# Attention kernel: differences by slot group, and sums of exponentials added up on VectorE before the denominators

## The chip, the cores and the metric

The kernel runs on one core of a Trainium2 chip. The metric is the device time of one execution in microseconds. The engines are named as in the profile: PE is the matrix engine (its weight loads are listed as PEld), DVE is VectorE, ACT is ScalarE, POOL is GpSimd and SP is the queue that issues most transfers.

## The reference

The whole program is a small audio layer. 128 batches of 64 features by 750 samples are pooled in windows of 8 to 94 tokens; then come a layer norm, an attention with 8 heads of width 8, and a feed-forward part with experts. The change lies in the attention alone. Cut to that:

```
qgr, _ = jnp.linalg.qr(q)
kgr, _ = jnp.linalg.qr(k)
attn_grass = jnp.einsum('bhnd,bhmd->bhnm', qgr, kgr) ** 2 * grassman_scale
dots = jnp.einsum('bhnd,bhmd->bhnm', q, k)
attn_eucl = dots * scale
attn_riem = dots ** 2 * riem_scale
a = jnp.concatenate([attn_eucl, attn_riem, attn_grass], axis=1)
...
a = jnp.einsum('oc,bcnm->bonm', conv_w, a) + conv_b[None, :, None, None]
a = jax.nn.softmax(a, axis=-1)
out = jnp.einsum('bhnm,bhmd->bhnd', a, v)
```

Three kinds of scores (24 channels) are mixed to 8, and a softmax over the keys follows. What matters here is the end of it: subtract a maximum, take exponentials, sum them over the keys (the denominators), multiply with v, and divide.

## The kernel before

The attention is the function `attend`. It works on pairs of batches, 64 pairs, one pair in a step. Each engine has its own program, written out by hand, and the five run beside each other; semaphores alone tie them. The order on each engine is that of its `step` function. PE's steps are all written out; the others have a loop of two steps a round.

The keys of a batch are laid out on 128 partitions (16 keys by 8 heads) in 6 slots, so the scores of a pair are `[128 partitions, 2 batches, 6 slots, 94 queries]`, all in f32. They lie in PSUM in `ps_a`, four banks: two for each batch, with slots 0 to 2 in one bank and 3 to 5 in the other. The parts of a step i are spread over three pairs:

- PE: `dots` of pair i in three groups (L1064), with `turn_keys` of pair i+2 (L1050) and `turn_max` of pair i-1 (L1071) behind the first group, `spread_max` of pair i-1 (L1077) behind the second, then `attended` (L1088) and `denominators` (L1095) of pair i-2, the third group, and `linear` (L1107) and `mixing` (L1115) of pair i, which fill `ps_a`.
- ACT: the squares of the dots (L1165), and between them the exponentials of pair i-1 (L1159 for slots 0 to 3, L1160 for slots 4 and 5, which has another bias), once for each batch.
- DVE: `maxima` of pair i-1 (`row_max`, L1188, once for each batch), `heads_max` (L1200, L1202), then the shift (L1206) and the two differences `prob` = `ps_a` - `shift` (L1211, one for each batch, 564 elements a partition), then `output` of pair i-2 (a reciprocal and a product, L1216 and L1218) and `key_blocks` of pair i+2 (L1195).
- POOL: `halves` (L1012) adds slots 0 to 2 to slots 3 to 5 of the exponentials of one pair, which leaves `half`, `[128, 2, 3, 94]`; then the key tiles (L1019, L1021), `m_blk` (L1005) and `v_blk` (L997).

The denominators are the sums over the partitions and over the three slots that are left. PE makes both in one: three matmuls a batch with `den_w`, which accumulate in PSUM. `linear` overwrites `ps_a`, so it waits for both differences of the pair before (`sub_done`).

Of the kernel before, what the change touches and what calls it, by code (L numbers as in the profile page):

```python
# [516 lines left out]
def later(c, behind):  # L517

    return not isinstance(c, int) or c >= behind
# [407 lines left out]
def attend(nc, q_cm, k_cm, m_t, o_cm, v_dram, k):  # L927
# [2 lines left out]
    SLOTS = 4  # L930
    with ExitStack() as ctx:
        names = ("m_ready keys_ready turned_ready mix_ready v_ready kt_done dots_done squared keyed mixed "
                 "max_done max_turned max_heads max_ready max_spread shift_done sub_done exp_done half_done av_done inv_done out_done")
        s = {n: ctx.enter_context(sem(n)) for n in names.split()}
        v_in = [ctx.enter_context(sem(f"v_in{a}")) for a in range(2)]
        q_in = [ctx.enter_context(sem(f"q_in{a}")) for a in range(2)]
# [14 lines left out]
        shift = sb("shift", [128, 2, N])  # L951
        prob = sb("prob", [128, 2, 2, NT, N])
        half = sb("half", [128, 2, 3, N])
        inv = sb("inv", [128, N])
        ps_dot = ctx.enter_context(nc.psum_tensor("ps_dot", [128, 3, 512], F32))
        ps_a = ctx.enter_context(nc.psum_tensor("ps_a", [128, 4, 512], F32))
        ps_m = ctx.enter_context(nc.psum_tensor("ps_m", [128, 512], F32))
        AV_AT, DEN_AT, KT_AT, REST = 0, N, 2 * N, 3 * N
        block = ctx.enter_context(nc.Block())

        def steps(eng, step):
# [28 lines left out]
        @block.gpsimd  # L990
        def _(pool):
            def values(j, a, n):
                pool.wait_ge(v_in[a], 32 * n)
                if later(j, 2):
                    pool.wait_ge(s["av_done"], j - 1)
                for b in range(2):
                    vb = pool.tensor_tensor(v_blk[:, a, b].rearrange("p t (o d) -> p (t o) d", o=H),  # L997
                                            v_rep[:, a, b].rearrange("p (t o d) -> p (t o) d", o=H, t=NT),
                                            k["vmask"][:].rearrange("p t o -> p (t o)").unsqueeze(2).broadcast_to([128, NT * H, D]), ALU.mult)
                vb.then_inc(s["v_ready"], 1)  # L1000

            def turning(i, a):
                if later(i, 2):
                    pool.wait_ge(s["kt_done"], i - 1)
                pool.tensor_tensor(m_blk[:, a], m_t[:, span(i, 1), :].broadcast_to([128, 16, D]),  # L1005
                                   k["mask16"][:].unsqueeze(2).broadcast_to([128, 16, D]), ALU.mult).then_inc(s["m_ready"], 1)

            def halves(j, a):
                pool.wait_ge(s["exp_done"], 2 * j + 2)
                if later(j, 1):  # L1010
                    pool.wait_ge(s["av_done"], j)
                pool.tensor_tensor(half[:], prob[:, a, :, 0:3, :], prob[:, a, :, 3:6, :], ALU.add).then_inc(s["half_done"], 1)  # L1012

            def build(i, a, n, has_next2):
                if later(i, 3):
                    halves(i - 3, 1 - a)
                if later(i, 2):
                    pool.wait_ge(s["keyed"], 2 * (i - 1))
                pool.tensor_tensor(k_blk[:, a, :, 0], k_cm[:, span(i, 1), :].rearrange("p i (u m) -> p (i u) m", m=4).unsqueeze(2).broadcast_to([128, NT * SLOTS, H, 4]),  # L1019
                                   k["hmask"][:].unsqueeze(1).unsqueeze(3).broadcast_to([128, NT * SLOTS, H, 4]), ALU.mult).then_inc(s["keys_ready"], 1)  # L1020
                pool.tensor_tensor(k_mix[:, a].rearrange("p t x o -> p (t x) o"), k_cm[:, span(i, 1), :].rearrange("p i m -> p (i m)").unsqueeze(2).broadcast_to([128, NP, H]),  # L1021
                                   k["conv1"].unsqueeze(1).broadcast_to([128, NP, H]), ALU.mult).then_inc(s["mix_ready"], 1)
                if has_next2:
                    turning(i + 2, a)
                if later(i, 1):
                    values(i - 1, 1 - a, n)

            turning(0, 0)
            turning(1, 1)
            for i in range(4):  # L1030
                build(i, i % 2, (i + 1) // 2, True)
            with pool.Fori(2, PAIRS // 2 - 1) as twice:
                build(2 * twice, 0, twice, True)
                build(2 * twice + 1, 1, twice + 1, True)
            build(PAIRS - 2, 0, PAIRS // 2 - 1, False)
            build(PAIRS - 1, 1, PAIRS // 2, False)
            halves(PAIRS - 3, 1)
            values(PAIRS - 1, 1, PAIRS // 2)
            halves(PAIRS - 2, 0)
            halves(PAIRS - 1, 1)  # L1040

        @block.tensor
        def _(pe):
# [45 lines left out]
                                  start=(t == 0), stop=(t == NT - 1), skip_group_check=True)  # L1089

            def denominators(j):
                pe.wait_ge(s["half_done"], j + 1)
                for t in range(3):
                    for b in range(2):
                        mm = pe.matmul(ps_m[64 * b:64 * b + 64, DEN_AT:DEN_AT + N], k["den_w"][:], half[:, b, t, :],  # L1095
                                       start=(t == 0), stop=(t == 2), skip_group_check=True)
                mm.then_inc(s["av_done"], 1)

            def linear(i, a):
                if later(i, 1):  # L1100
                    pe.wait_ge(s["sub_done"], 2 * i)
                pe.wait_ge(s["mix_ready"], i + 1)
                for t in range(NT):
                    for b in range(2):
                        for w in range(2):
                            half_of = slice(64 * w, 64 * w + 64)
                            mm = pe.matmul(ps_a[half_of, 2 * b + t // 3, N * (t % 3):N * (t % 3) + N],  # L1107
                                           k_mix[64 * b:64 * b + 64, a, t, 8 * w:8 * w + 8].rearrange("p x o -> p (x o)"), q_st[64 * b:64 * b + 64, a, :],
                                           start=(t % 3 == 0), stop=False, skip_group_check=True)
                        if t == NT - 1:  # L1110
                            mm.then_inc(s["keyed"], 1)

            def squares_mixed(i, b, v):
                for c in range(SLOTS):
                    mm = pe.matmul(ps_a[32 * c:32 * c + 32, 2 * b + v, 0:3 * N], k["mix_w"][64 * v:64 * v + 64, :],  # L1115
                                   sq[64 * v:64 * v + 64, b, c].rearrange("p t n -> p (t n)"), start=False, stop=True, skip_group_check=True)
                return mm

# [35 lines left out]

        @block.scalar
        def _(act):
            def exps(prev, a, b):
                act.wait_ge(s["sub_done"], 2 * prev + b + 1)
                act.activation(prob[:, a, b, 0:4], prob[:, a, b, 0:4], ACT.Exp, bias=k["head_const"][:])  # L1159
                act.activation(prob[:, a, b, 4:6], prob[:, a, b, 4:6], ACT.Exp, bias=k["pad_bias"][:]).then_inc(s["exp_done"], 1)  # L1160

            def squares(i, g):
                act.wait_ge(s["dots_done"], 3 * i + g + 1)
                for b in range(2):
                    act.activation(sq[:, b, :, g, :], ps_dot[:, (2 * g + b) % 3, 0:SLOTS * N].rearrange("p (c n) -> p c n", c=SLOTS),  # L1165
                                   ACT.Square).then_inc(s["squared"], 1)

            def step(i, a, has_prev, has_prev2, has_next2):
                if has_prev:
                    act.wait_ge(s["mixed"], 2 * i)  # L1170
                squares(i, 0)
                squares(i, 1)
                if has_prev:
                    exps(i - 1, 1 - a, 0)
                squares(i, 2)
                if has_prev:
                    exps(i - 1, 1 - a, 1)

            steps(act, step)
            for b in range(2):  # L1180
                exps(PAIRS - 1, 1, b)

        @block.vector
        def _(dve):
# [19 lines left out]
            def shifted(prev, a):  # L1204
# [2 lines left out]
                dve.wait_ge(s["shift_done"], prev + 1)  # L1207
                if later(prev, 2):
                    dve.wait_ge(s["av_done"], prev - 1)
                for b in range(2):  # L1210
                    dve.tensor_tensor(prob[:, a, b].rearrange("p (v t) n -> p v t n", v=2), bass.AP(ps_a[:].tensor, 1024 * b, [[4 * 512, 128], [512, 2], [N, 3], [1, N]]),  # L1211
                                      shift[:, b, :].unsqueeze(1).unsqueeze(1).broadcast_to([128, 2, 3, N]), ALU.subtract).then_inc(s["sub_done"], 1)

            def output(j):
                dve.wait_ge(s["av_done"], j + 1)
# [4 lines left out]
            def step(i, a, has_prev, has_prev2, has_next2):  # L1220
                if has_prev:
                    maxima(i - 1)
                if has_prev:
                    heads_max(i - 1)
                    shifted(i - 1, 1 - a)
                if has_prev2:
                    output(i - 2)
# [6 lines left out]
            maxima(PAIRS - 1)  # L1234
            heads_max(PAIRS - 1)
            shifted(PAIRS - 1, 1)
            output(PAIRS - 2)
            output(PAIRS - 1)


def finish(nc, h, o_cm, out, k):
# [288 lines left out]
```

## Time and profile before

| | us |
|---|---|
| median of 3 runs | 924.77 |
| lowest and highest | 920.41, 924.92 |
| the profiled execution, in all | 921.8 |
| its span in the trace | 920.1 |
| the attention, first to last `row_max` in the trace | 316.1 to 781.7 |

The profile is of one execution. It lists each engine's busy time, the groups of instructions by line with what ended the idle time before them, and a timeline. Durations are those of single instructions; consecutive instructions on an engine can overlap by some hundredths of a microsecond. A matmul of f32 is recorded as two passes, so 6 matmuls stand there as x12. "128x94 f32<-128x564 f32" reads output and input, partitions by elements.

### The profile page before, as it was taken

The page shows a single profiled execution, that of the slowest core. Times are in us where ns is not written, and L with a number is a line of the kernel's source. Part 1 is how long each engine was busy: PE and PEld are TensorE (multiplying, and loading weights), DVE is VectorE, ACT ScalarE, POOL GpSimd, SP SyncE. Part 2 cuts the span into 40 slices and gives each one's busy share as a digit, 9 for nine tenths or more (in the row PEclk, how much of TensorE's full clock was granted, in tenths as well). Part 3 has the DMA queues.
Part 4 walks back from the last instruction along what each step waited for, and adds up shares of the span by engine and source line. Part 5 has one row for each costly group of instructions (what it writes and reads, how often), then busy time and mean ns, then how long its engine had stood idle before and what let it go on. Part 6 is the DMA issues. An engine that isn't in the chain of part 4 may idle for free. (4 is left out here: it accounts for less than half of the span.)

```text
span 920.1 us, 40061 instructions
## 1 busy us (share of the span) xinstructions
PE 812.1 (88%) x16806; PEld 580.0 (63%) x16806; DVE 678.7 (74%) x1163; ACT 452.4 (49%) x966; POOL 506.6 (55%) x551
## 2 busy tenths in 40 slices
PE   3577768899895699999999999999999999699994
PEld 2233325455553577887888877777888877366663
DVE  4488894488799577777787877777787877377772
ACT  2233333211282265555565655555565655277773
POOL 3256570121000688888888888888888886222220
PEclk9678888799998699999999999999999999799998
DMA  8667200022410122222111222222221111001111
GB/s 291 264 219 250 69 1 0 12 60 50 113 48 0 60 62 63 65 71 66 61 61 62 61 62 63 67 68 66 61 62 61 61 62 42 1 18 28 29 28 33
DMA packets 64293, 64.92 MB, mean 71 GB/s; under 512 B 36825, under 2 KB 54812, under 8 KB 64156
## 3 DMA queue, kind: packets, MB, share of 16 engines
q1 hardware_dynamic: 63628, 61.24, 21.4%
q8 instruction: 124, 2.03, 0.9%
q10 hardware_dynamic: 528, 1.54, 0.5%
q14 instruction: 13, 0.11, 0.0%
HBM read 52.93 MB, written 6.75 MB: 65 GB/s over the span
## 5 line engine op out<-in xcount | busy, mean ns | idle before, releaser
L1165 ACT ACTIVATE sq<-ps_dot 128x376 f32<-128x376 f32 x384 | 165.2, 483 | 160.5 <-PE ps_dot L1064 160.5
L1064 PE MATMUL ps_dot<-q_st,k_blk 64*64 64x94 f32 x6144 | 170.5, 249 | 1.1 <-ACT sq L1165 0.8
L1064 PEld LDWEIGHTS ps_dot<-q_st,k_blk 64*64 64x64 f32 x6144 | 134.6, 134 | 53.0 <-issue 28.8
L997 POOL TENSOR_TENSOR v_blk<-v_rep,vmask 128x384 f32<-128x384 f32 x128 | 106.6, 854 | 27.4 <-PE ps_m L1095 27.4
L1012 POOL TENSOR_TENSOR half<-prob 128x564 f32<-128x564 f32 x64 | 75.6, 1181 | 61.0 <-ACT prob L1160 61.0
L1188 DVE TENSOR_REDUCE row_max<-ps_a 128x94 f32<-128x564 f32 x128 | 89.4, 740 | 24.0 <-PE ps_a L1115 24.0
L1159 ACT ACTIVATE prob<-prob,head_const 128x376 f32<-128x376 f32 x128 | 78.0, 609 | 57.0 <-DVE prob L1211 57.0
L1019 POOL TENSOR_TENSOR k_blk<-k_cm,hmask 128x768 f32<-128x768 f32 x64 | 96.8, 1513 | 1.0 <-PE ps_a L1107 1.0
L1021 POOL TENSOR_TENSOR k_mix<-k_cm,cols 128x768 f32<-128x768 f32 x64 | 96.8, 1513 | 0.0
L1211 DVE TENSOR_TENSOR prob<-ps_a,shift 128x564 f32<-128x564 f32 x128 | 89.4, 740 | 4.9
L367 PE MATMUL ps_spread<-parts,pair_sel 128*128 128x376 bf16 x256 | 58.1, 368 | 34.7 <-DVE prod L477 22.8
L1115 PE MATMUL ps_a<-sq,mix_w 64*32 64x282 f32 x2048 | 82.0, 404 | 0.1
L436 POOL TENSOR_TENSOR prod<-x_g,w_odd 128x752 f32<-128x752 f32 x32 | 56.9, 1778 | 39.1 <-ACT w_odd L419 39.1
L1088 PE MATMUL ps_m<-prob,v_blk 128*64 128x94 f32 x1536 | 76.6, 248 | 1.5 <-ACT prob L1160 1.5
L1107 PE MATMUL ps_a<-q_st,k_mix 64*64 64x94 f32 x3072 | 74.8, 241 | 1.2 <-DVE prob L1211 0.9
L1297 POOL COPY w_sel<-ffn_w 128x258 f32 x64 | 25.8, 403 | 87.9 <-issue 73.5
L1088 PEld LDWEIGHTS ps_m<-prob,v_blk 128*64 128x64 f32 x1536 | 64.7, 136 | 8.6 <-ACT prob L1160 1.7
L1107 PEld LDWEIGHTS ps_a<-q_st,k_mix 64*64 64x64 f32 x3072 | 67.4, 133 | 1.8 <-DVE prob L1211 1.0
L1195 DVE TENSOR_TENSOR k_blk<-ps_m,hmask 128x768 f32<-128x768 f32 x64 | 61.3, 958 | 7.5 <-PE ps_dot L1064 4.9
L367 PEld LDWEIGHTS ps_spread<-parts,pair_sel 128*128 128x128 bf16 x256 | 23.4, 106 | 65.6 <-issue 30.3
L468 DVE TENSOR_REDUCE tokens<-prod 128x94 f32<-128x752 f32 x64 | 57.1, 927 | 7.3 <-POOL prod L436 6.9
L1005 POOL TENSOR_TENSOR m_blk<-m_t,mask 128x128 f32<-128x128 f32 x64 | 25.9, 405 | 58.0 <-POOLq L731 58.0
(225 smaller groups left out, 1408.0 us busy)
## 6 DMA issues: line engine op xcount, KB each, us to landing
v_rep<-v_rows SPq DMA_DIRECT2D x128, 192.0 KB, 3.0
x_g<-in_x_dram SPq DMA_DIRECT2D x15, 1500.0 KB, 6.6
v_rows<-tok SPq DMA_DIRECT2D x16, 192.0 KB
q_st<-q_cm SPq DMA_DIRECT2D x64, 47.0 KB, 1.8
out_dram<-rows SPq DMA_DIRECT2D x16, 188.0 KB
x_g<-in_x_dram ACTq DMA_DIRECT2D x1, 1500.0 KB, 7.6
top_rows<-tok SPq DMA_DIRECT2D x16, 32.0 KB
top<-top_rows SPq DMA_DIRECT2D x1, 512.0 KB, 3.4
```

What stands on the lines that cost most here:

```text
L367: mm = pe.matmul(ps_spread[:, 2 * (n % 2) + half, 0:HALF], k["pair_sel"][:, half, n, :], parts[:, a, part, :], start=(part == 0), stop=(pa ...
L997: vb = pool.tensor_tensor(v_blk[:, a, b].rearrange("p t (o d) -> p (t o) d", o=H), v_rep[:, a, b].rearrange("p (t o d) -> p (t o) d", o=H, ...
L1019: pool.tensor_tensor(k_blk[:, a, :, 0], k_cm[:, span(i, 1), :].rearrange("p i (u m) -> p (i u) m", m=4).unsqueeze(2).broadcast_to([128, NT ...
L1021: pool.tensor_tensor(k_mix[:, a].rearrange("p t x o -> p (t x) o"), k_cm[:, span(i, 1), :].rearrange("p i m -> p (i m)").unsqueeze(2).broa ...
L1064: mm = pe.matmul(ps_dot[64 * v:64 * v + 64, (2 * g + b) % 3, N * c:N * c + N], k_blk[rows, a, SLOTS * (3 * v + g) + c].rearrange("p k h m ...
L1088: pe.matmul(ps_m[64 * b:64 * b + 64, AV_AT:AV_AT + N], v_blk[:, a, b, t, :], prob[:, a, b, t, :], start=(t == 0), stop=(t == NT - 1), skip ...
L1107: mm = pe.matmul(ps_a[half_of, 2 * b + t // 3, N * (t % 3):N * (t % 3) + N], k_mix[64 * b:64 * b + 64, a, t, 8 * w:8 * w + 8].rearrange("p ...
L1115: mm = pe.matmul(ps_a[32 * c:32 * c + 32, 2 * b + v, 0:3 * N], k["mix_w"][64 * v:64 * v + 64, :], sq[64 * v:64 * v + 64, b, c].rearrange(" ...
L1159: act.activation(prob[:, a, b, 0:4], prob[:, a, b, 0:4], ACT.Exp, bias=k["head_const"][:])
L1165: act.activation(sq[:, b, :, g, :], ps_dot[:, (2 * g + b) % 3, 0:SLOTS * N].rearrange("p (c n) -> p c n", c=SLOTS), ACT.Square).then_inc(s ...
L1188: dve.tensor_reduce(top[:, b, :], bass.AP(ps_a[:].tensor, 1024 * b, [[4 * 512, 128], [1, N], [512, 2], [N, 3]]), AX.XY, ALU.max).then_inc( ...
L1211: dve.tensor_tensor(prob[:, a, b].rearrange("p (v t) n -> p v t n", v=2), bass.AP(ps_a[:].tensor, 1024 * b, [[4 * 512, 128], [512, 2], [N, ...
```

## The change

Three things change in `attend`.

1. The difference is taken by slot group in place of by batch: first slots 0 to 2 of both batches in one instruction (564 elements), then slots 3 to 5 of each batch (282 each). For that the two banks of batch 0 trade places (`BANK`). The exponentials follow the same groups: slots 0 to 2 of both batches, then slot 3 of both and slots 4 and 5 of both, three instructions where there were four. `linear` waits for the first group's difference before its first slot and for the other two before its fourth.
2. A new step on DVE, `summed`, adds the three slots of `half` to one, `sums`, `[128, 2, 94]`, with a reduction whose innermost axis is the slot. It stands behind `heads_max` and ahead of the shift.
3. The denominators are one matmul a batch on `sums`, two in all where there were six. They wait for `sums_done` in place of `half_done`, and so do POOL's `halves`, in place of `av_done`.

```diff
+        sums = sb("sums", [128, 2, N])
...
+        BANK = ((1, 0), (2, 3))
...
                 if later(j, 1):
-                    pool.wait_ge(s["av_done"], j)
+                    pool.wait_ge(s["sums_done"], j)
                 pool.tensor_tensor(half[:], prob[:, a, :, 0:3, :], prob[:, a, :, 3:6, :], ALU.add).then_inc(s["half_done"], 1)
...
             def denominators(j):
-                pe.wait_ge(s["half_done"], j + 1)
-                for t in range(3):
-                    for b in range(2):
-                        mm = pe.matmul(ps_m[64 * b:64 * b + 64, DEN_AT:DEN_AT + N], k["den_w"][:], half[:, b, t, :],
-                                       start=(t == 0), stop=(t == 2), skip_group_check=True)
+                pe.wait_ge(s["sums_done"], j + 1)
+                for b in range(2):
+                    mm = pe.matmul(ps_m[64 * b:64 * b + 64, DEN_AT:DEN_AT + N], k["den_w"][:], sums[:, b, :],
+                                   start=True, stop=True, skip_group_check=True)
                 mm.then_inc(s["av_done"], 1)
...
             def linear(i, a):
-                if later(i, 1):
-                    pe.wait_ge(s["sub_done"], 2 * i)
                 pe.wait_ge(s["mix_ready"], i + 1)
                 for t in range(NT):
+                    if later(i, 1) and t % 3 == 0:
+                        pe.wait_ge(s["sub_done"], 3 * i - 2 + 2 * (t // 3))
...
-            def exps(prev, a, b):
-                act.wait_ge(s["sub_done"], 2 * prev + b + 1)
-                act.activation(prob[:, a, b, 0:4], prob[:, a, b, 0:4], ACT.Exp, bias=k["head_const"][:])
-                act.activation(prob[:, a, b, 4:6], prob[:, a, b, 4:6], ACT.Exp, bias=k["pad_bias"][:]).then_inc(s["exp_done"], 1)
+            def exps(prev, a, v):
+                act.wait_ge(s["sub_done"], 3 * prev + 2 * v + 1)
+                if v == 0:
+                    act.activation(prob[:, a, :, 0:3], prob[:, a, :, 0:3], ACT.Exp, bias=k["head_const"][:]).then_inc(s["exp_done"], 1)
+                else:
+                    act.activation(prob[:, a, :, 3], prob[:, a, :, 3], ACT.Exp, bias=k["head_const"][:])
+                    act.activation(prob[:, a, :, 4:6], prob[:, a, :, 4:6], ACT.Exp, bias=k["pad_bias"][:]).then_inc(s["exp_done"], 1)
...
+                dve.tensor_tensor(prob[:, a, :, 0:3], bass.AP(ps_a[:].tensor, 512 * BANK[0][0], [[4 * 512, 128], [512, 2], [N, 3], [1, N]]),
+                                  shift[:].unsqueeze(2).broadcast_to([128, 2, 3, N]), ALU.subtract).then_inc(s["sub_done"], 1)
                 for b in range(2):
-                    dve.tensor_tensor(prob[:, a, b].rearrange("p (v t) n -> p v t n", v=2), bass.AP(ps_a[:].tensor, 1024 * b, [[4 * 512, 128], [512, 2], [N, 3], [1, N]]),
-                                      shift[:, b, :].unsqueeze(1).unsqueeze(1).broadcast_to([128, 2, 3, N]), ALU.subtract).then_inc(s["sub_done"], 1)
+                    dve.tensor_tensor(prob[:, a, b, 3:6], ps_a[:, BANK[b][1], 0:3 * N].rearrange("p (t n) -> p t n", t=3),
+                                      shift[:, b, :].unsqueeze(1).broadcast_to([128, 3, N]), ALU.subtract).then_inc(s["sub_done"], 1)
+
+            def summed(j):
+                dve.wait_ge(s["half_done"], j + 1)
+                if later(j, 1):
+                    dve.wait_ge(s["av_done"], j)
+                dve.tensor_reduce(sums[:], half[:].rearrange("p b t n -> p b n t"), AX.X, ALU.add).then_inc(s["sums_done"], 1)
...
                 if has_prev:
                     heads_max(i - 1)
+                if has_prev2:
+                    summed(i - 2)
+                if has_prev:
                     shifted(i - 1, 1 - a)
```

DVE in the second step of a round of its loop, from the reduction of the turned maxima to the product of `output`. Before:

```order
L1200 TENSOR_REDUCE row_max_o<-ps_a 94x16 [waits max_turned]
L1202 TENSOR_REDUCE row_max_e<-row_max_o 94x256 [waits max_heads]
L1206 TENSOR_SCALAR shift<-ps_a,head_const 128x188 [waits max_spread]
L1211 TENSOR_TENSOR prob<-ps_a,shift 128x564 [waits av_done,shift_done]
L1211 TENSOR_TENSOR prob<-ps_a,shift 128x564
L1216 RECIPROCAL inv<-ps_m 128x94 [waits av_done]
L1218 ISA [waits inv_done]
L1218 TENSOR_TENSOR q_cm<-ps_m,inv 128x94
```

The same place after the change:

```order
L1204 TENSOR_REDUCE row_max_o<-ps_a 94x16 [waits max_turned]
L1206 TENSOR_REDUCE row_max_e<-row_max_o 94x256 [waits max_heads]
L1224 TENSOR_REDUCE sums<-half 128x188 [waits av_done,half_done]
L1210 TENSOR_SCALAR shift<-ps_a,head_const 128x188 [waits max_spread]
L1214 TENSOR_TENSOR prob<-ps_a,shift 128x2x282 [waits av_done,shift_done]
L1217 TENSOR_TENSOR prob<-ps_a,shift 128x282 x2
L1228 RECIPROCAL inv<-ps_m 128x94 [waits av_done]
L1230 ISA [waits inv_done]
L1230 TENSOR_TENSOR q_cm<-ps_m,inv 128x94
```

One reduction is new between `row_max_e` and the shift, and the second of the two differences is now two.

PE in the same steps, from the attended matmuls to `linear`. Before:

```order
L1088 MATMUL ps_m<-prob,v_blk 64x94 [waits out_done,v_ready,exp_done]
L1088 MATMUL ps_m<-prob,v_blk 64x94 x11
L1095 MATMUL ps_m<-half,den_w 64x94 [waits half_done]
L1095 MATMUL ps_m<-half,den_w 64x94 x5
L1064 MATMUL ps_dot<-q_st,k_blk 64x94 [waits squared]
L1064 MATMUL ps_dot<-q_st,k_blk 64x94 x15
L1107 MATMUL ps_a<-q_st,k_mix 64x94 [waits mix_ready,sub_done]
L1107 MATMUL ps_a<-q_st,k_mix 64x94 x23
```

After the change:

```order
L1090 MATMUL ps_m<-prob,v_blk 64x94 [waits out_done,v_ready,exp_done]
L1090 MATMUL ps_m<-prob,v_blk 64x94 x11
L1096 MATMUL ps_m<-sums,den_w 64x94 [waits sums_done]
L1096 MATMUL ps_m<-sums,den_w 64x94
L1066 MATMUL ps_dot<-q_st,k_blk 64x94 [waits squared]
L1066 MATMUL ps_dot<-q_st,k_blk 64x94 x15
L1108 MATMUL ps_a<-q_st,k_mix 64x94 [waits sub_done,mix_ready]
L1108 MATMUL ps_a<-q_st,k_mix 64x94 x11
L1108 MATMUL ps_a<-q_st,k_mix 64x94 [waits sub_done]
L1108 MATMUL ps_a<-q_st,k_mix 64x94 x11
```

The denominators are two matmuls where there were six, and `linear` has a second wait in its middle.

## Rows read from the trace of the kernel before

**Rows 1.** The page, part 1: busy us, share of the span, instructions.

```profile
PE 812.1 (88%) x16806; PEld 580.0 (63%) x16806; DVE 678.7 (74%) x1163; ACT 452.4 (49%) x966; POOL 506.6 (55%) x551
```

**Rows 2.** One loop step: length, PE, PEld, DVE, ACT, POOL busy, PEclk, DMA share, GB/s.

```profile
522.08:529.44 7.36, 7.27 (x231) 5.92 (x218) 5.86 (x10) 4.36 (x10) 6.15 (x6) 1.00 0.21 62
```

**Rows 3.** Timeline of DVE, that step: start us, us, instruction, [idle before, its releaser].

```profile
522.08 1.40 DVE L1188 TENSOR_REDUCE row_max<-ps_a 128x94 f32<-128x564 f32 x2 [0.25 <-PE ps_a L1115]
523.95 0.42 DVE L1200 TENSOR_REDUCE row_max_o<-ps_a 94x16 f32<-94x256 f32 x1 [0.47 <-PE ps_a L1071]
524.40 0.42 DVE L1202 TENSOR_REDUCE row_max_e<-row_max_o 94x256 f32<-94x256 f32 x1
525.29 0.41 DVE L1206 TENSOR_SCALAR shift<-ps_a,head_const 128x188 f32<-128x188 f32 x1 [0.48 <-PE ps_a L1077]
525.74 1.40 DVE L1211 TENSOR_TENSOR prob<-ps_a,shift 128x564 f32<-128x564 f32 x2
527.05 0.73 DVE L1216 RECIPROCAL inv<-ps_m 128x94 f32<-128x94 f32 x1
527.94 0.26 DVE L1218 TENSOR_TENSOR q_cm<-ps_m,inv 128x94 f32 x1
528.15 0.96 DVE L1195 TENSOR_TENSOR k_blk<-ps_m,hmask 128x768 f32<-128x768 f32 x1
529.44 0.74 DVE L1188 TENSOR_REDUCE row_max<-ps_a 128x94 f32<-128x564 f32 x1 [0.34 <-PE ps_a L1115]
```

**Rows 4.** Timeline of PE and one instruction of ACT in the same step.

```profile
524.87 0.38 PE L1077 MATMUL ps_a<-ident,row_max_e 94*128 94x94 f32 x2
525.18 1.20 PE L1088 MATMUL ps_m<-prob,v_blk 128*64 128x94 f32 x24
526.21 0.66 PE L1095 MATMUL ps_m<-half,den_w 128*64 128x94 f32 x12
526.80 0.88 PE L1064 MATMUL ps_dot<-q_st,k_blk 64*64 64x94 f32 x32
527.49 1.15 PE L1107 MATMUL ps_a<-q_st,k_mix 64*64 64x94 f32 x48
528.57 1.28 PE L1115 MATMUL ps_a<-sq,mix_w 64*32 64x282 f32 x32
...
527.74 0.86 ACT L1165 ACTIVATE sq<-ps_dot 128x376 f32<-128x376 f32 x2 [0.27 <-PE ps_dot L1064]
```

**Rows 5.** DVE by line, 330 to 760 us: busy us, mean ns, idle before.

```profile
L1188 DVE TENSOR_REDUCE row_max<-ps_a 128x94 f32<-128x564 f32 x118 | 82.4, 740 | 18.9 <-PE ps_a L1115 18.9
L1211 DVE TENSOR_TENSOR prob<-ps_a,shift 128x564 f32<-128x564 f32 x116 | 81.0, 740 | 4.6
...
L1200 DVE TENSOR_REDUCE row_max_o<-ps_a 94x16 f32<-94x256 f32 x58 | 24.4, 421 | 27.0 <-PE ps_a L1071 27.0
L1202 DVE TENSOR_REDUCE row_max_e<-row_max_o 94x256 f32<-94x256 f32 x58 | 24.1, 416 | 2.0
...
L1218 DVE TENSOR_TENSOR q_cm<-ps_m,inv 128x94 f32 x58 | 14.9, 256 | 8.7
```

**Rows 6.** DVE by line, whole span: reads of SBUF, contiguous and with steps.

```profile
L468 DVE TENSOR_REDUCE tokens<-prod 128x94 f32<-128x752 f32 x64 | 57.1, 927 | 7.3 <-POOL prod L436 6.9
...
L814 DVE TENSOR_TENSOR head_rows<-aug,rs 128x1024 f32<-128x1024 f32 x1 | 2.7, 2710 | 0.0
...
L240 DVE TENSOR_REDUCE batch_sel<-ident 128x1 f32<-128x64 f32 x2 | 0.4, 220 | 0.1
...
L228 DVE TENSOR_REDUCE delta<-delta_q 128x8 f32<-128x128 f32 x1 | 0.4, 383 | 0.0
```

**Rows 7.** Two stretches of 10 us ahead of the attention: PE busy, PEclk, DMA share, GB/s.

```profile
60.00:70.00 10.00, 8.53 (x53) 0.58 0.71 236
...
280.00:290.00 10.00, 8.54 (x50) 1.00 0.00 0
```

More of the change, by code:

```diff
@@ L932, in attend @@
         names = ("m_ready keys_ready turned_ready mix_ready v_ready kt_done dots_done squared keyed mixed "
-                 "max_done max_turned max_heads max_ready max_spread shift_done sub_done exp_done half_done av_done inv_done out_done")
+                 "max_done max_turned max_heads max_ready max_spread shift_done sub_done exp_done half_done sums_done av_done inv_done out_done")
         s = {n: ctx.enter_context(sem(n)) for n in names.split()}
@@ L1106, in linear @@
                             half_of = slice(64 * w, 64 * w + 64)
-                            mm = pe.matmul(ps_a[half_of, 2 * b + t // 3, N * (t % 3):N * (t % 3) + N],
+                            mm = pe.matmul(ps_a[half_of, BANK[b][t // 3], N * (t % 3):N * (t % 3) + N],
                                            k_mix[64 * b:64 * b + 64, a, t, 8 * w:8 * w + 8].rearrange("p x o -> p (x o)"), q_st[64 * b:64 * b + 64, a, :],
@@ L1114, in squares_mixed @@
                 for c in range(SLOTS):
-                    mm = pe.matmul(ps_a[32 * c:32 * c + 32, 2 * b + v, 0:3 * N], k["mix_w"][64 * v:64 * v + 64, :],
+                    mm = pe.matmul(ps_a[32 * c:32 * c + 32, BANK[b][v], 0:3 * N], k["mix_w"][64 * v:64 * v + 64, :],
                                    sq[64 * v:64 * v + 64, b, c].rearrange("p t n -> p (t n)"), start=False, stop=True, skip_group_check=True)
@@ L1179, in _ @@
             steps(act, step)
-            for b in range(2):
-                exps(PAIRS - 1, 1, b)
+            for v in range(2):
+                exps(PAIRS - 1, 1, v)
         @block.vector
@@ L1236, in _ @@
             shifted(PAIRS - 1, 1)
-            output(PAIRS - 2)
-            output(PAIRS - 1)
+            for j in (PAIRS - 2, PAIRS - 1):
+                summed(j)
+                output(j)
 def finish(nc, h, o_cm, out, k):
```

## The prediction

> **What bounds the kernel now.** I read the page's busy shares first, then the attention stage step by step, since every edit lies there. The page says PE is busy 88% of the span and DVE 74% [rows 1]. That is an average over stages with different limits, so I took the window of one step of the steady loop, from one start of `row_max` to the next: 7.36 us long, PE busy 7.27 us, DVE 5.86, POOL 6.15, ACT 4.36, clock 1.00 [rows 2]. PE fills the step, and the other four engines wait for it or for each other. The timeline of DVE in the same step shows where DVE stands still: 0.47 us for the transposes of the maxima (L1071), 0.48 us for the spread maxima (L1077), and 0.34 us for the mixing matmuls (L1115) that feed the next `row_max` [rows 3]. Those three waits, 1.29 us, are all the slack that DVE has, and only what they leave can be filled with new work. Over the 58 steps between 330 and 760 us the grouped rows show the same: 18.9 us idle before `row_max` and 27.0 before `row_max_o`, 0.33 and 0.47 us a step [rows 5]. The mean step over this stretch is 430/58.2, about 7.39 us, a little above the step in the window, because a few steps are late; I use 7.39 for before.
>
> So two rings lie close together. On PE: from the spread of the maxima at 524.87 through attended, denominators, the third dots, linear and mixing to the next `row_max` at 529.44 [rows 3, 4]. On DVE: its own instructions in order, plus the waits that it can't fill.
>
> **What the change takes from PE.** The denominators go from 6 matmuls to 2; the trace shows each as two passes, x12 now, x4 then. From the start of the 12 at 526.21 to the start of the dots behind them at 526.80 are 0.59 us [rows 4], 0.049 us a pass. Eight passes fewer are 0.39 us a step. PE's ring alone would then be 7.39 - 0.39 = 7.00 us.
>
> **What the change gives to DVE.** (a) The wider difference: two instructions of 564 elements become one of 564 and two of 282. `prob` and `row_max` in pairs of 564 take 1.40 us for 2 x 0.74 [rows 3, 5], so each starts 0.66 us after the one before, 0.08 less than it lasts. Between the 564 elements of L1211 at 740 ns and the 94 of L1218 at 256 ns lie 1.03 ns an element [rows 5]; so 282 take 0.45 us, 0.37 start to start. Three are 0.66 + 0.37 + 0.37 = 1.40 against 1.32: +0.08 us. (b) The new `sums` reduction, W. It is 564 elements on 128 partitions, like `row_max`. If it costs as `row_max` does, W is 0.74 us.
>
> DVE's ring then, per step: busy 5.86, plus the wait for L1071 of 0.47 that stays (DVE has nothing to do between `row_max` and `row_max_o`; `sums` stands behind `row_max_e`), plus small gaps of 0.08, 0.15 and 0.03 before the difference, the product and `row_max_e` [rows 3, 5]: 6.59. The 0.48 us wait for the spread is gone, since `sums` fills it: `row_max_e` ends at 524.82, the spread is there at 525.29 [rows 3], and any W above 0.47 covers that. The 0.34 us wait for mixing also goes as soon as DVE is the later one. Where a wait goes, the neighbours overlap by 0.08, at three places. So the ring is 6.59 + 0.08 + W - 0.24 = 6.43 + W; I round to 6.45 + W. Against 7.39 now, **the point of no change is W = 0.94 us**: below it the change gains, above it DVE sets the step and it loses.
>
> **What W is.** The input of `sums` is `half` in SBUF, read with the three slots innermost: 94 f32 elements, 376 bytes, from one element to the next, then one element on. `row_max` walks the same steps, but in PSUM, so its 0.74 says nothing of SBUF. Rows of VectorE on SBUF: contiguous, 752 elements in 927 ns (L468), so 1.03 ns each and some 150 ns fixed; a step of 8 bytes, 64 elements in 220 ns (L240), 1.1 ns each; a reduction with an innermost step of 32 bytes, 128 elements in 383 ns (L228), 1.82 ns each; and L814, a product whose first operand is `aug` turned, innermost step 96 bytes and then one element on, 1024 elements in 2710 ns, 2.50 ns each [rows 6]. At 1.03 ns W is 0.74 us, at 1.82 it is 0.15 + 564 x 1.82 ns = 1.18 us, at 2.50 it is 1.56 us. The walk of `sums` is nearest to the last: both make a far step at every element and come back one element on, and the cost grew from 8 to 32 to 96 bytes. I take **1.56 us** and keep 0.74 and 1.18 for the range. Nothing excludes more, since 376 bytes lie beyond every row.
>
> The Trainium skill (SBUF — State Buffer, in the section Door 1: The DMA port swizzle) says that SBUF is read in lines of 16 bytes, that full rate needs at least two accesses in each line, and that every change of line costs something. That speaks against this change. The trace agrees that 8 bytes are free and 32 are not, but the rule makes no difference between 32 and 96 bytes, while the rows do (1.82 against 2.50 ns); by the rule the 1.18 us of L228 would hold, by the row 1.56.
>
> **The other edits.** They cost nothing while the following covers last. ACT does one exp of 564 elements and two smaller ones where it had four: with 0.27 us of idle time before L1165 and 4.36 us of work in 7.36, it has room [rows 2, 4]. Its first exp waits for the first difference, which at W = 1.56 lands near 5.3 us into the step; the third squares can follow at 6.2 and mixing at 6.7, ready for `row_max` at about 7.6, before the 8.0 at which DVE comes. POOL's halves wait for `sums_done` in place of `av_done`, both of the step before. PE's denominators wait for `sums`: it ends 2.7 + 1.56 = 4.2 us into the step, and the attended matmuls end at 526.38, 4.3 us in [rows 4], so even this W is just hidden there. The second half of linear (the new wait before the fourth slot) starts at about 6.1 instead of 5.4 at the latest; mixing still comes before DVE needs it. The renamed banks move no work.
>
> **The sum.** 60 steps have the full ring. Each goes from 7.39 to 6.45 + 1.56 = 8.01: +0.62, +37.2 us. The last two steps have no key blocks on DVE; there the path by difference, second half of linear and mixing is longer, and they lose some 0.25 us each. Behind the loop two more reductions lie open, one largely beside the last exps, for about 1 us. In all +39 us on the profiled execution's 921.8: 960.5, and I say **960 us**. The median of before is 924.8, 3 us above the profiled one; I let that stand as noise inside the range.
>
> **Rivals.**
> First, **the milder step cost**: W = 1.18 at the price of L228, which is the same operation. The ring is 7.63, +0.24 x 60 + 1 = +15: 937 us. For it: the operation. Against it: its step is 12 times shorter than that of `sums`.
> Second, **no step cost, faster**: W = 0.74. The DVE ring is 7.19, PE's 7.00, so DVE binds but below 7.39: -0.20 x 60 = -12, 910 us. It decides for W below 0.94. For it: `row_max` with the same walk at full rate in PSUM, and that only three streams are read, each of them returning to its neighbour element. Against it: both strided SBUF rows. The Trainium skill (VectorE: DVE Perf Modes, The perf-mode tier table) gives tensor_reduce one rate wherever its f32 operand lies; by that the step would be this one.
> Third, **PE loses its clock**. With DVE as the bound PE idles 8.01 - 6.88 = 1.1 us in each step, busy 86%. Earlier in this trace, one stretch of 10 us with PE busy 8.53 had a clock of 0.58, another with 8.54 had 1.00 [rows 7]. If the granted clock fell from 2.4 to 1.2 GHz in even a tenth of the loop, PE would need up to twice its 6.88 us there: about +5.9 us in each of 6 steps, +35 more, 995 us.
> Fourth, **the change doesn't matter**: W close to 0.94, 920 to 929 us; no row points there.
>
> **Chances.** 1.56 or near it, 950 to 972 us: 48%. The milder cost, 930 to 949: 26%. No step cost: 12%, faster. Near 0.94: 4%. A lost clock or a W beyond 1.75, above 975: 10%. Faster by more than 0.5%: 0.12; within 0.5%, about what a measurement of this kernel can tell from none: 0.05; slower: 0.83. The range 929 to 976 us holds the first two and what lies between and around them, nearly 8 in 10.
>
> **What would show it.** In the profile after: `sums` at about 1.56 us a piece (1.18 or 0.74 for the rivals); the 12 passes of denominators are 4; no idle time before the shift (L1077's wait gone) and none before `row_max`; DVE's busy share in the loop from 80% to over 93%, PE's from 99% to about 86%; PE waiting at L1071 and in linear for DVE; from one first `row_max` to the next 8.0 us; clock still 1.00. I am wrong if `sums` is below 0.94 us, or if DVE still waits somewhere that I have called filled.

## The result and the profile after

The changed kernel takes 909.33 us (median of 4 runs, 908.78 to 910.35) against 922.59 for the kernel before beside it: a ratio of 0.987, interval 0.984 to 0.989. It is faster by 13 us, where 38 us slower were forecast. The profiled execution took 910.35 us with a span of 908.7.

One step of the loop after the change, from one start of `row_max` to the next. The columns are those of [rows 2]: length, busy time of PE, PEld, DVE, ACT and POOL, clock, DMA share, GB/s.

```profile
523.02:530.20 7.18, 7.04 (x222) 5.64 (x210) 6.49 (x13) 4.17 (x9) 6.25 (x7) 1.00 0.21 64
```

DVE works 6.49 us of the step where it worked 5.86, and PE 7.04 where it worked 7.27. The timeline of DVE in this step answers [rows 3]:

```profile
523.02 1.39 DVE L1192 TENSOR_REDUCE row_max<-ps_a 128x94 f32<-128x564 f32 x2
524.81 0.42 DVE L1204 TENSOR_REDUCE row_max_o<-ps_a 94x16 f32<-94x256 f32 x1 [0.41 <-PE ps_a L1073]
525.27 0.42 DVE L1206 TENSOR_REDUCE row_max_e<-row_max_o 94x256 f32<-94x256 f32 x1
525.61 0.79 DVE L1224 TENSOR_REDUCE sums<-half 128x188 f32<-128x564 f32 x1
526.31 0.40 DVE L1210 TENSOR_SCALAR shift<-ps_a,head_const 128x188 f32<-128x188 f32 x1
526.75 0.74 DVE L1214 TENSOR_TENSOR prob<-ps_a,shift 128x564 f32<-128x564 f32 x1
527.41 0.80 DVE L1217 TENSOR_TENSOR prob<-ps_a,shift 128x282 f32<-128x282 f32 x2
528.13 0.73 DVE L1228 RECIPROCAL inv<-ps_m 128x94 f32<-128x94 f32 x1
529.01 0.26 DVE L1230 TENSOR_TENSOR q_cm<-ps_m,inv 128x94 f32 x1
529.33 0.96 DVE L1199 TENSOR_TENSOR k_blk<-ps_m,hmask 128x768 f32<-128x768 f32 x1
530.20 1.39 DVE L1192 TENSOR_REDUCE row_max<-ps_a 128x94 f32<-128x564 f32 x2
```

Of the three waits in [rows 3] one is left, 0.41 us before `row_max_o`. The waits before the shift and before `row_max` are gone, as DVE is now the later one at both places. The reduction of the sums took 0.79 us, not 1.56. Grouped over 330 to 760 us, as [rows 5] (busy us, mean ns, idle before):

```profile
L1192 DVE TENSOR_REDUCE row_max<-ps_a 128x94 f32<-128x564 f32 x122 | 84.6, 735 | 0.9 <-PE ps_a L1116 0.8
...
L1217 DVE TENSOR_TENSOR prob<-ps_a,shift 128x282 f32<-128x282 f32 x120 | 48.0, 442 | 0.0
L1224 DVE TENSOR_REDUCE sums<-half 128x188 f32<-128x564 f32 x60 | 47.5, 792 | 0.0
...
L1204 DVE TENSOR_REDUCE row_max_o<-ps_a 94x16 f32<-94x256 f32 x60 | 25.3, 421 | 24.7 <-PE ps_a L1073 24.7
```

The idle time before `row_max` fell from 18.9 us to 0.9. How long the loop takes in all is read from the first and last start of `row_max`, here of before and then of after (duration in ns min/median/max, first and last start in us):

```profile
L1188 DVE TENSOR_REDUCE row_max<-ps_a x128: 732/742/746, 316.1 to 781.7; 128x94 f32<-128x564 f32 x128
```

```profile
L1192 DVE TENSOR_REDUCE row_max<-ps_a x128: 734/735/746, 315.9 to 766.4; 128x94 f32<-128x564 f32 x128
```

465.6 us became 450.5, so a mean step, a sixty-third of it, went from 7.39 to 7.15 us. (Both are 0.01 us high, since the last start is that of the pair's second reduction.) That is 15.1 us, more than the 11.4 by which the two spans differ. The rest was given back behind the loop: from the last `row_max` to the end are 138.4 us before and 142.3 after. Two windows of each show why, first before, then after (columns as above):

```profile
781.70:792.00 10.30, 5.39 (x78) 3.78 (x78) 5.76 (x12) 1.79 (x4) 2.21 (x3) 1.00 0.01 2
792.00:805.00 13.00, 10.24 (x15) 3.51 (x16) 3.76 (x4) 3.94 (x7) 2.81 (x7) 0.50 0.00 0
```

```profile
766.40:778.00 11.60, 6.90 (x61) 5.40 (x62) 6.87 (x14) 1.67 (x3) 1.77 (x2) 0.58 0.00 0
778.00:790.00 12.00, 8.78 (x12) 2.51 (x10) 4.18 (x4) 2.82 (x4) 3.21 (x8) 0.50 0.01 1
```

The drain is the stretch in which the last pairs leave the engines, from the last `row_max` to the first matmul of the feed-forward part: 8.97 us before (781.70 to 790.67) and 11.02 after (766.40 to 777.42). In both kernels PE idles for parts of it, while the last differences and exponentials are made, and its granted clock falls to the lower level. Before, it had the upper level until 792 us, when the drain was over, and was low for the 13.6 us from there; after, it fell at 768.3, within the drain, and was low for 27.1 us. The last attended matmuls took longer for it:

```profile
773.56 2.15 PE L1090 MATMUL ps_m<-prob,v_blk 128*64 128x94 f32 x24 [1.23 <-DVE q_cm L1230]
```

Those 24 passes take 1.20 us in [rows 4]. So 2.05 of the 3.9 us were lost in the drain and the other 1.85 in the feed-forward part behind it, where the two kernels do the same work.

### The profile page after: what moved, and what is told of

Read it like the earlier page. It is cut to its first block and busy times, and to the rows that moved or that the text cites. A ratio compares the mean times of both kernels' runs of the same rounds, so it can differ in the third digit from the quotient of the medians.

```text
span 908.7 us, 39105 instructions
## 1 busy us (share of the span) xinstructions
PE 798.0 (88%) x16294; PEld 564.3 (62%) x16294; DVE 719.1 (79%) x1291; ACT 439.6 (48%) x902; POOL 506.5 (56%) x551
## 5 line engine op out<-in xcount | busy, mean ns | idle before, releaser
L1161 ACT ACTIVATE prob<-prob,head_const 128x564 f32<-128x564 f32 x64 | 49.1, 768 | 67.0 <-DVE prob L1214 67.0
L1090 PE MATMUL ps_m<-prob,v_blk 128*64 128x94 f32 x1536 | 78.5, 252 | 1.2 <-DVE q_cm L1230 1.2
L600 POOL TENSOR_TENSOR rstd_of<-rstd_t,pair_mask 128x384 f32<-128x384 f32 x16 | 13.2, 826 | 72.3 <-PE ps_rstd L654 44.3
```

What stands on the lines that cost most here:

```text
L1090: pe.matmul(ps_m[64 * b:64 * b + 64, AV_AT:AV_AT + N], v_blk[:, a, b, t, :], prob[:, a, b, t, :], start=(t == 0), stop=(t == NT - 1), skip ...
```

## The experiments

Each kernel was compared with the kernel before on the same chip. "Step" is the time from the first to the last start of `row_max`, divided by 63. The two kernels with a measuring block (1 and 2) ran once each; their times in all say nothing, and every row of the block stands twice in the trace, alike within 0.01 us.

**1. What a step in SBUF costs.** A block behind the end of the kernel before holds single VectorE instructions on one tile. `walk(n, s, k)` reads k elements at a distance of s elements, then moves on by one element (or by m, in the second block), n times.

```diff
+            def walk(n, s, k):
+                return bass.AP(field[:].tensor, 0, [[4096, 128], [1, n], [s, k]])
...
+                step(dve.tensor_reduce(out["line"][:], walk(188, 8, 3), AX.X, ALU.add))
...
+                step(dve.tensor_reduce(out["ninety"][:], walk(188, 24, 3), AX.X, ALU.add))
...
+                step(dve.tensor_reduce(out["pitch"][:], walk(188, 94, 3), AX.X, ALU.add))
...
+                step(dve.tensor_reduce(out["eight"][:], walk(70, 24, 8), AX.X, ALU.add))
+                step(dve.tensor_reduce(out["eightfar"][:], walk(70, 94, 8), AX.X, ALU.add))
+                step(dve.tensor_reduce(out["sixteen"][:], walk(35, 8, 16), AX.X, ALU.add))
```

> The kernel before, with a block behind its end that only measures: single VectorE reductions and products over one SBUF tile, each at its own line, twice. Disputed is why the reduction of the sums, with 376 bytes from one element to the next, took 0.79 us where the steps of 32 and 96 bytes of two earlier rows had led to 1.18 and 1.56. Theory A, the number of places in one turn decides: three places an element apart from their last visit stay cheap at any step (all reductions of 188 x 3 elements 0.73 to 0.80 us, at 16, 32, 64, 96, 128, 376, 384 and 1024 bytes alike), and eight or sixteen places are dear (8 x 70 at 96 and at 376 bytes both near 1.5 us, 16 x 35 at 32 bytes near 1.2). Theory B, the length of the step decides, whatever the number: 3 x 188 at 32 bytes 1.2 us, at 96 bytes 1.5 us, at 376 bytes 0.79 us, and 8 x 70 at 376 bytes 0.75 us. The product of 1024 elements at 96 bytes is 2.7 us by both, at 376 bytes 2.7 by A and 1.2 by B.

Timeline of the block (start us, us), once through: a plain read of 564 elements, 3 places with steps of 32, 96 and 376 bytes, then 8 places at 96 and 376 bytes, 16 at 32, and two products of 1024 elements, the first operand read in 8 places at 96 and 376 bytes.

```profile
926.10 0.74 DVE L1457 TENSOR_REDUCE w_flat<-field 128x188 f32<-128x564 f32 x1
...
927.65 0.80 DVE L1459 TENSOR_REDUCE w_line<-field 128x188 f32<-128x564 f32 x1
...
929.32 0.80 DVE L1461 TENSOR_REDUCE w_ninety<-field 128x188 f32<-128x564 f32 x1
...
930.99 0.80 DVE L1463 TENSOR_REDUCE w_pitch<-field 128x188 f32<-128x564 f32 x1
...
933.49 1.50 DVE L1466 TENSOR_REDUCE w_eight<-field 128x70 f32<-128x560 f32 x1
935.03 1.15 DVE L1467 TENSOR_REDUCE w_eightfar<-field 128x70 f32<-128x560 f32 x1
936.21 1.15 DVE L1468 TENSOR_REDUCE w_sixteen<-field 128x35 f32<-128x560 f32 x1
937.40 2.62 DVE L1469 TENSOR_TENSOR w_turned<-field 128x1024 f32<-128x1024 f32 x1
940.05 1.98 DVE L1470 TENSOR_TENSOR w_turnedfar<-field 128x1024 f32<-128x1024 f32 x1
```

Three places cost 0.80 us at every step from 32 bytes on; a step of 1024 bytes gave the same, and 16 bytes 0.74. Theory B falls. Theory A holds in kind, and missed two sizes: at 8 places 376 bytes are cheaper than 96, in the reduction (1.15 against 1.50) and in the product (1.98 against 2.62), so the step has a part once there are many places. The prices read from [rows 6] were right for their own walks: 16 places at 32 bytes come to 1.79 ns an element here and the product at 96 bytes to 2.41, where the rows had 1.82 and 2.50.

**2. Where it begins, and whether the coming back matters.**

```diff
+                step(dve.tensor_reduce(out["three"][:], walk(188, 94, 3), AX.X, ALU.add))
+                step(dve.tensor_reduce(out["four"][:], walk(141, 94, 4), AX.X, ALU.add))
...
+                step(dve.tensor_reduce(out["line"][:], walk(188, 94, 3, 4), AX.X, ALU.add))
...
+                step(dve.tensor_reduce(out["stream"][:], walk(188, 4, 3, 12), AX.X, ALU.add))
+                step(dve.tensor_reduce(out["streamnear"][:], walk(188, 2, 3, 6), AX.X, ALU.add))
```

> The kernel before with a second measuring block behind its end. The first block showed 3 places at 0.80 us whatever the step from 32 to 1024 bytes, 8 places at 376 bytes 1.15, 8 at 96 bytes 1.50 and 16 at 32 bytes 1.15 us. Open: where between 3 and 8 places the cost begins, and whether it is the coming back to a neighbour element that keeps three places cheap. Theory A, a few places are remembered: 2 and 3 places at 376 bytes 0.75 to 0.80 us, a jump to 1.15 somewhere from 4 to 8; with three places but 32 or 64 bytes between one turn and the next (nothing comes back to a neighbour) 1.2 us or more, and a plain stream with a step of 32 bytes 1.2 us too. Theory B, only the number of places in a turn counts, not the coming back: three places stay at 0.80 us even at 64 bytes from turn to turn, and so does the plain stream read in threes.

Timeline: 2, 3, 4, 5, 6 and 8 places at 376 bytes; then 3 places at 376 bytes that move on by 16, 32 and 64 bytes a turn, and two plain streams with steps of 16 and 8 bytes.

```profile
925.92 0.74 DVE L1455 TENSOR_REDUCE w_two<-field 128x282 f32<-128x564 f32 x1
926.70 0.80 DVE L1456 TENSOR_REDUCE w_three<-field 128x188 f32<-128x564 f32 x1
927.53 1.11 DVE L1457 TENSOR_REDUCE w_four<-field 128x141 f32<-128x564 f32 x1
928.67 1.13 DVE L1458 TENSOR_REDUCE w_five<-field 128x112 f32<-128x560 f32 x1
929.84 1.18 DVE L1459 TENSOR_REDUCE w_six<-field 128x94 f32<-128x564 f32 x1
...
932.29 1.15 DVE L1461 TENSOR_REDUCE w_eight<-field 128x70 f32<-128x560 f32 x1
...
936.45 1.17 DVE L1464 TENSOR_REDUCE w_line<-field 128x188 f32<-128x564 f32 x1
937.66 1.15 DVE L1465 TENSOR_REDUCE w_pair<-field 128x188 f32<-128x564 f32 x1
938.84 1.10 DVE L1466 TENSOR_REDUCE w_apart<-field 128x188 f32<-128x564 f32 x1
939.97 1.14 DVE L1467 TENSOR_REDUCE w_stream<-field 128x188 f32<-128x564 f32 x1
941.15 0.74 DVE L1468 TENSOR_REDUCE w_streamnear<-field 128x188 f32<-128x564 f32 x1
```

The jump lies between three places (0.80) and four (1.11). Three places are cheap only as long as each visit comes back close to the last: moved on by 16 bytes a turn they cost 1.17, by 32 and 64 bytes 1.15 and 1.10. So theory B falls here too, and theory A holds, with times a little under its 1.2. A plain stream costs nothing extra at 8 bytes and 1.14 us at 16. These rows are as if VectorE held the last three places it read, each up to the next 16 bytes. That is a reading and not shown: it says nothing of the 1.50 us at 96 bytes in the first block, nor of why 16 bytes between three places cost 0.74 and 32 bytes 0.80. The Trainium skill (SBUF — State Buffer, in the section Door 1: The DMA port swizzle) says that SBUF has lines of 16 bytes and that a second access in a line is what makes full rate; the two streams agree with that. Its penalty for each change of line, which the prediction drew on, does not fit `w_three`: there every access changes the line and the whole costs 0.06 us more than a plain read, and the measurement decides.

**3. Was DVE's ring the right ring?** The reduction is made twice.

```diff
+                dve.tensor_reduce(spare[:], half[:].rearrange("p b t n -> p b n t"), AX.X, ALU.add)
                 dve.tensor_reduce(sums[:], half[:].rearrange("p b t n -> p b n t"), AX.X, ALU.add).then_inc(s["sums_done"], 1)
```

> The changed kernel with the reduction of the sums made twice, the first into a tile that nothing reads. It makes DVE's own work 0.72 us a step longer (0.79 less the overlap of 0.07). Theory: DVE's ring sets the step after the change, so the prediction's ring was right and only W was wrong: 7.2 becomes 7.9 us, 909 becomes 909 + 62 x 0.72 = 954 us. Rival: PE's ring sets the step and DVE has slack (PE 7.0, DVE less): under 930 us.

953.32 us (952.18 to 955.18), 1.035 times before, interval 1.032 to 1.038. The step is 7.85 us, 0.70 more than after the change, for one reduction of 0.80 us that starts 0.71 before the next. The clock over 330 to 760 us stayed at its upper level, with PE busy 416 of 430 us:

```profile
330.00:760.00 430.00, 415.82 (x11478) 317.25 (x11474) 394.12 (x713) 222.18 (x492) 337.19 (x330) 1.00 0.19 60
```

Ahead of `row_max`, where DVE of the kernel before waited 18.9 us, it waits for nothing here:

```profile
L1193 DVE TENSOR_REDUCE row_max<-ps_a 128x94 f32<-128x564 f32 x110 | 76.3, 735 | 0.0
```

So DVE's ring does set the step, and had one reduction cost 1.56 us, the kernel would have been slower, near what was forecast: here the two add 1.50 us (0.79 and 0.71), and 953 us were measured where 960 were forecast at 1.56.

**4. Is it the matmuls that gain?** Six matmuls on PE beside the sums.

```diff
-                for b in range(2):
-                    mm = pe.matmul(... sums[:, b, :], ...)
+                for t in range(3):
+                    for b in range(2):
+                        mm = pe.matmul(... sums[:, b, :], ...)
```

> The changed kernel with each denominator matmul issued three times, so six on PE as before the change (the result is the same), while VectorE still adds the sums. Theory: PE's ring goes back to 7.39 us and passes DVE's 7.2: 921 us, as before the change. Rival, the gain comes from the finer waits (difference by slot group, linear starting on the first group): 909 to 912 us, as PE would not be what binds.

924.21 us (922.03 to 928.23), ratio 1.004, interval 1.002 to 1.005. The loop takes 465.6 us, a step of 7.39, the same as before to the last digit: with its passes back PE binds again, and the rival, that the finer waits make the gain, falls. The 3 us over the expected 921 lie outside the loop.

**5. The two parts apart.** First the grouping alone, with `denominators` and `halves` as before and no `summed`:

```diff
-                if has_prev2:
-                    summed(i - 2)
```

> One part alone: differences, exponentials and linear's waits by slot group as in the changed kernel, but no sums on VectorE and six matmuls of denominators on half. Theory: no wait of linear was last before, so grouping buys nothing: 922 us, and 920 to 924 holds. Rival, that grouping is a part of the gain: 912 to 918 us.

920.65 us (917.48 to 922.78), ratio 0.999, interval 0.998 to 1.000; step 7.39. DVE's added 0.07 us a step came out of its wait for mixing, which fell from 18.9 to 15.0 us:

```profile
L1193 DVE TENSOR_REDUCE row_max<-ps_a 128x94 f32<-128x564 f32 x118 | 82.4, 740 | 15.0 <-PE ps_a L1117 15.0
```

Then the sums alone, with the differences by batch:

```diff
+                if has_prev2:
+                    summed(i - 2)
+                if has_prev:
                     shifted(i - 1, 1 - a)
```

> The other part alone: the sums on VectorE and two matmuls of denominators, but differences and exponentials by batch as before, and linear waiting for both of them. DVE's ring is 0.08 us shorter than in the changed kernel (two differences instead of three), 7.1 us; but linear waits for the whole difference, which ends 0.26 us later than in the kernel before, while PE arrives 0.39 us earlier. In the kernel before PE reached linear 0.35 us after the difference was done, so PE now waits some 0.3 us there and its path from the difference over linear and mixing to row_max comes last: mixing's first half is done 7.3 us after row_max. Theory: the grouping is what lets the gain through: 914 to 920 us. Rival: DVE's own ring stays last and the grouping buys nothing: 904 to 908 us.

915.85 us (915.12 to 918.42), ratio 0.994, interval 0.992 to 0.996; step 7.27, and here the weight loads of `linear` wait for the difference:

```profile
PEld ps_a L1107 <- DVE prob L1211: 10.3, 59, 0.2
```

(waiting engine and line, what it waited for, us in total, times, longest). So the sums alone give about half of the gain (7.3 of the loop's 15.1 us), and the grouping, which is worth nothing by itself, lets the other half through: the second half of `linear` is all that still has to wait for the last difference, and in the changed kernel no wait of `linear` for a difference is left in the loop. The grouping also changed the exponentials, from four instructions to three; that part was not tried by itself.

**6. The saving on PE without the reduction.** The grouping with two matmuls that read one slot of `half` and no reduction.

```diff
-                pe.wait_ge(s["sums_done"], j + 1)
+                pe.wait_ge(s["half_done"], j + 1)
                 for b in range(2):
-                    mm = pe.matmul(... sums[:, b, :], ...)
+                    mm = pe.matmul(... half[:, b, 0, :], ...)
```

> The changed kernel without the reduction of the sums: the two matmuls of denominators read slot 0 of half alone, so the output leaves out two thirds of each denominator. It asks what the saving of matmuls is worth when DVE pays nothing for it. Theory: DVE's ring falls well below PE's, and the step is PE's ring, 7.39 less 0.39 = 7.0 us: 897 us. Rival, another path is just behind: 902 us or more.

904.39 us (900.82 to 905.05), ratio 0.981, interval 0.977 to 0.985; step 7.08 where 7.00 was expected. The rival named at 902 us or more is the one that holds: another path is just behind. DVE's ring did not fall well below PE's:

```profile
L1192 DVE TENSOR_REDUCE row_max<-ps_a 128x94 f32<-128x564 f32 x122 | 84.9, 738 | 2.9 <-PE ps_a L1116 2.8
...
L1210 DVE TENSOR_SCALAR shift<-ps_a,head_const 128x188 f32<-128x188 f32 x61 | 25.3, 414 | 29.0 <-PE ps_a L1079 29.0
```

With the reduction gone the wait for the spread maxima is back, 29.0 us in 61 steps or 0.48 a step, and before `row_max` DVE waits 0.05 us a step. In the prediction's own terms this ring is 6.59 + 0.08 for the third difference + 0.48 for the spread - 0.08 of overlap at `row_max` = 7.07 us. PE's is 7.39 less the 0.33 us that the matmuls turned out to save (below), 7.06. The two are level at the measured 7.08, so this kernel does not part them. And it says why a reduction of 0.79 us costs only 0.07 us a step, about 4 us in all: most of it lies in a wait that DVE would have had anyway.

**7. The shift on ScalarE.** It follows from 3 and 6 that 0.07 us a step can be had by taking work from DVE, and ACT has room.

```diff
+            def spread_shift(prev):
+                act.wait_ge(s["max_spread"], prev + 1)
+                act.activation(shift[:], bass.AP(ps_a[:].tensor, 512 + REST, [[4 * 512, 128], [1024, 2], [1, N]]), ACT.Identity,
+                               bias=k["head_const"][:]).then_inc(s["shift_done"], 1)
...
-                dve.wait_ge(s["max_spread"], prev + 1)
-                dve.tensor_scalar(shift[:], ... k["head_const"][:], None, ALU.add).then_inc(s["shift_done"], 1)
```

`spread_shift` is called between the two squares of the second group.

> The changed kernel with the shift (the spread maxima plus a constant, copied from PSUM) made by ScalarE between the two squares of the second group instead of by VectorE. VectorE's work falls by 0.43 us a step; the difference can then start when ScalarE is done: spread there at 526.12, one activation of 188 elements some 0.35 us, so at about 526.5 instead of 526.75. Theory (two rings, DVE's last at 7.2 and PE's at 7.0): the step falls to about 7.0, as PE takes over, so 897 to 902 us. Rival: ScalarE's later squares delay the third dots or mixing, or the trip over ScalarE takes longer than DVE's own 0.43: 908 us or more.

902.6 us (902.27 to 903.17), ratio 0.980, interval 0.977 to 0.983: the lowest median here, some 7 us below the changed kernel and just above the 897 to 902 expected. The step is 7.08 us, the same as without any reduction, and DVE again waits only 0.05 us a step before `row_max` (3.0 us in 61 steps): the two rings are level again. The timeline, DVE and ACT around the shift:

```profile
521.79 0.79 DVE L1230 TENSOR_REDUCE sums<-half 128x188 f32<-128x564 f32 x1
...
522.35 0.42 ACT L1168 ACTIVATE shift<-ps_a,head_const 128x188 f32<-128x188 f32 x1
522.66 0.48 ACT L1176 ACTIVATE sq<-ps_dot 128x376 f32<-128x376 f32 x1
522.79 0.75 DVE L1220 TENSOR_TENSOR prob<-ps_a,shift 128x564 f32<-128x564 f32 x1 [0.21 <-ACT shift L1168]
```

The shift runs beside the sums, and the difference starts 0.21 us after their end, where it was 0.35 (526.40 to 526.75 in the changed kernel). ACT's activation took 0.42 us, not the 0.35 expected.

## Why the prediction was wrong

- **What binds, and the point of no change: right.** PE's ring of 7.39 and DVE's close behind it, the three waits and which of them would go, the cover of `sums` by the spread's round trip: all are as read from [rows 2 to 5]. Six matmuls bring the step back to 7.39 (experiment 4), a doubled reduction lengthens it by 0.70 (experiment 3), and without the reduction the wait for the spread is back at 0.48 (experiment 6).
- **PE's saving: right in kind, 0.06 us too large.** The timeline of PE in the changed kernel, at the place of [rows 4]:

```profile
527.08 0.33 PE L1096 MATMUL ps_m<-sums,den_w 128*64 128x94 f32 x4
527.34 0.88 PE L1066 MATMUL ps_dot<-q_st,k_blk 64*64 64x94 f32 x32
```

  From start to start that is 0.26 us where 0.59 were, 0.33 less instead of 0.39. The prediction divided the 0.59 us by all 12 passes; by the two measured groups a pass is worth 0.041 us, and some 0.1 us of a group does not shrink with them (an estimate from 0.59 for 12 and 0.26 for 4). PE's ring alone is then 7.06 us, not 7.00. Experiment 6 has a step shorter by 0.31 us.
- **The ring's sum: right in kind, 0.09 us high.** 6.45 + W with the measured 0.79 gives 7.24; measured were 7.15. Of it 0.06 are the wait before `row_max_o`, 0.41 where I kept 0.47, and 0.02 the rounding from 6.43.
- **W: wrong, and this alone turned the sign.** The step that failed is "The walk of `sums` is nearest to the last: both make a far step at every element and come back one element on". I ordered the rows by the length of their step. L228 has 16 places in a turn and L814 has 8; `sums` has 3, and three places are read almost at full rate whatever the step (experiments 1 and 2: 0.80 at 32 to 1024 bytes, 1.11 with a fourth place). The milder price, 1.18 us from L228, was too high as well. The prediction also says that `row_max` "walks the same steps", and this is not so: it reads six places in turn, three slots in each of two banks of PSUM. Six places 376 bytes apart in SBUF took 1.18 us (`w_six`; its own steps were not tried there), so its 0.74 says nothing of SBUF and lies within 0.05 us of `sums` by chance; it was right to set it aside. The second rival had the argument in its other half ("only three streams are read, each of them returning to its neighbour element"), at a chance of 12%. Its time, 910 us, is hit in part by luck: the step fell by 0.24 us where it took 0.20, the loop by 15.1 us where it took 12, and the 3.9 us lost behind the loop, for which it counted nothing, made up for that.
- **The other edits: right for the grouping alone, wrong in the company of the sums.** By itself it changes nothing (experiment 5), but without it the sums give 6 us and not 13. The prediction named no worth for it, since at W = 1.56 it would have had none.
- **The clock: the third rival did not come in the loop, where its condition was not met.** It took PE to idle 1.1 us a step; at 7.15 against PE's own 7.06 it is about 0.1. Nearest to the condition is experiment 3, at 7.85 against 7.06, and there the clock stayed at its upper level. By the prediction's reckoning PE would be busy 6.88 of 7.85 us there, 88%, and the profile lists 97%, so its busy share does not show how much slack PE has. Behind the loop, for which the rival had nothing, the clock fell earlier than before, and that and the two reductions that the drain has gained gave back 3.9 of the loop's 15.1 us; the prediction had about 1 us for the reductions. Experiment 6, without them and with the clock low from within the drain as well, has a drain of 9.68 us against 11.02, so some 1.3 us go with the reductions and the other 2.6 with the clock (an estimate from single executions).

## What to carry to other kernels

Before pricing a strided read of SBUF by a row with strides, count the places that it visits in turn and whether each visit comes back close to the last: up to three such places went at almost full rate here, and with a fourth the same 564 elements took 50% longer than a plain read. Take the row from the same memory: six places in turn took 0.74 us in PSUM and 1.18 in SBUF. When two engines' rings lie within a few tenths of a microsecond of each other, work that leaves one must not cost the other more than its waits; write down the ring of each and the cost at which the sign turns, and put most of the effort into the number on which the sign hangs. Work can be nearly free where it fills a wait of its engine, and taking it out again then brings the wait back. And a wait for a whole result may be worth splitting only after something else has moved: grouping gave nothing alone and half of the gain together.

## What was not expected of the hardware

- VectorE reads three separate places of SBUF in turn at 0.80 us for 564 f32 elements where a plain read takes 0.74, and four places at 1.11 us, with 376 bytes between them. From PSUM `row_max` reads six places in turn at 0.74 us.
- With eight places, a distance of 96 bytes (1.50 us for 560 elements) is dearer than 376 (1.15). The cause is open.
- Behind the dense loop PE's granted clock fell at different points of nearly the same drain and stayed at the low level for 13.6 us before the change and 27.1 after it, which moved the end by some microseconds.
